# Two message layers of a graph network on one core: who waits for copied rows and added sums, when a half tile's own rows are copied, and where unused rows are cleared

## What is computed

```python
h = x @ W_enc.T + b_enc
row, col = (edge_index[0], edge_index[1])
for l in range(2):                                  # the two message layers
    m = jnp.concatenate([h[row], h[col]], axis=-1)
    m = jax.nn.relu(m @ msg_W1[l].T + msg_b1[l])
    m = m @ msg_W2[l].T + msg_b2[l]
    agg = jax.ops.segment_sum(m, col, num_segments=h.shape[0])
    upd = jnp.concatenate([h, agg], axis=-1) @ upd_W[l].T + upd_b[l]
    h = _layer_norm(h + upd, ln_g[l], ln_b[l])
return h @ W_out.T + b_out
```

## Time and profile before

| | |
|---|---|
| median of the runs | 3340.25 us |
| the profiled execution: span from its first to its last instruction | 3302.9 us |
| the median less that span (what lies around it) | 37.35 us |
| message layer 0, first and second pass | 626.3 to 911 us, 915.5 to 1254 us |
| message layer 1, first and second pass | 1360.7 to 1646 us, 1650.7 to 1990 us |
| TensorE matmuls busy | 2918.4 us (88%) |
| VectorE busy | 2503.1 us (76%) |
| ScalarE busy | 2057.0 us (62%) |
| GpSimd busy | 703.6 us (21%) |
| granted TensorE clock over the span | 0.934 of full speed |

### The profile page before, as it was taken

One profiled execution on the slowest core, in us unless ns is written; L12 is line 12 of the kernel. 1 busy time (PEld: TensorE's weight loads), 2 busy tenths in 40 slices (PEclk: granted clock), 3 DMA queues, 4 the chain that ended last, 5 costly groups with the idle time before them and its releaser, 6 DMA issues.

```text
span 3302.9 us, 219046 instructions
## 1 busy us (share of the span) xinstructions
PE 2918.4 (88%) x88775; PEld 2722.9 (82%) x88775; DVE 2503.1 (76%) x4764; ACT 2057.0 (62%) x3886; POOL 703.6 (21%) x909
## 2 busy tenths in 40 slices
PE   3666665799999998799999997799999899999999
PEld 3555454699989997699989996699999799999999
DVE  8999999777767776677777775689899855565555
ACT  1433333677767776777767774677777555555555
POOL 2222123400011117200011116244444300000000
PEclk7777776999999999899999998799999999999999
DMA  3000000566656762466667663155555488868888
GB/s 74 7 6 6 6 6 20 179 186 182 189 167 185 190 183 68 142 186 187 185 171 188 185 182 56 50 180 183 182 183 184 147 262 265 265 214 246 272 262 252
DMA packets 409174, 518.87 MB, mean 157 GB/s; under 512 B 157279, under 2 KB 280709, under 8 KB 409095
## 3 DMA queue, kind: packets, MB, share of 16 engines
q1 hardware_dynamic: 395757, 498.98, 51.0%
q0 software_dynamic: 4000, 8.20, 2.2%
q10 hardware_dynamic: 9338, 10.73, 1.1%
HBM read 408.98 MB, written 108.72 MB: 157 GB/s over the span
## 4 chain that ended last, share of the span: by engine, by line
PE 70%; DVE 13%; issue 7%; DMA 4%; POOL 3%; ACT 2%; SPq 0%; DVEq 0%; POOLq 0%; ACTq 0%
PE psum L1349 19%; PE psum L1583 17%; PE psum L1367 9%; PE psum L1353 9%; PE psum L1570 6%; PE psum L1550 3%; PE psum L703 1%; DMA tabf<-in_x 1%; PE psum L1558 1%; DMA cells_kept<-arena 1%; DVE Hf L943 1%; DVE Hf L1082 1%; DMA arena<-rows_far,ovcur 1%; DVE Hf L2144 1%; POOL arena L2057 1%
## 5 line engine op out<-in xcount | busy, mean ns | idle before, releaser
L1349 PE MATMUL psum<-tabf,arena 125*32 125x128 f16 x40256 | 1091.8, 220 | 27.9 <-DVE arena L1445 16.0
L1353 PE MATMUL psum<-arena 96*32 96x128 f16 x20928 | 1027.5, 221 | 7.4 <-issue 7.4
L1349 PEld LDWEIGHTS psum<-tabf,arena 125*32 125x32 f16 x40256 | 949.8, 98 | 91.4 <-issue 45.0
L1400 ACT ACTIVATE arena<-psum 128x512 f32<-128x512 f32 x1300 | 775.2, 596 | 340.4 <-PE psum L1353 339.5
L1353 PEld LDWEIGHTS psum<-arena 96*32 96x32 f16 x20928 | 690.5, 95 | 7.7 <-issue 7.7
L1583 PE MATMUL psum<-tabr,cellr 125*125 125x256 f32 x5000 | 623.4, 285 | 6.2 <-ACT cellr L1502 6.0
L1583 PEld LDWEIGHTS psum<-tabr,cellr 125*125 125x125 f32 x5000 | 606.4, 187 | 7.1 <-issue 7.1
L1367 PE MATMUL psum<-arena 128*32 128x129 f32 x10400 | 565.9, 277 | 1.4 <-issue 1.4
L1502 ACT CAST cellr<-arena 125x630 fp32r<-125x630 f16 x500 | 359.7, 720 | 267.4 <-PE psum L1583 255.8
L1502 DVE CAST cellr<-arena 125x630 fp32r<-125x630 f16 x500 | 244.0, 488 | 241.3 <-PE psum L1583 236.0
L1612 ACT CAST arena<-psum 125x500 f16<-125x500 f32 x625 | 356.6, 578 | 100.7 <-PE psum L1550 46.0
(11 more groups left out here) (313 smaller groups left out, 4444.9 us busy)
## 6 DMA issues: line engine op xcount, KB each, us to landing
arena<-cells_kept SPq DMA_DIRECT2D x500, 315.0 KB, 3.5
cells_kept<-arena SPq DMA_DIRECT2D x625, 126.0 KB
arena<-slots_turned_from SPq DMA_DIRECT2D x152, 384.0 KB
tabf<-slots_turned_from SPq DMA_DIRECT2D x150, 384.0 KB, 4.0
arena<-slots_turned_from SPq DMA_DIRECT2D x50, 512.0 KB
tabf<-slots_turned_from SPq DMA_DIRECT2D x50, 512.0 KB
arena<-slots_turned_to SPq DMA_DIRECT2D x152, 96.0 KB
tabf<-slots_turned_to SPq DMA_DIRECT2D x150, 96.0 KB, 4.3
```

The costliest lines, as they stand in the source:

```text
L1349: pe.matmul(psCell[b][q:q + GW, g * D:(g + 1) * D], fr, rows, start=g == 0 and p == 0, stop=False, tile_position=(0, q), skip_group_check= ...
L1353: m = pe.matmul(psCell[b][q:q + GW, g * D:(g + 1) * D], toB[part][:, here + q:here + q + GW], cur[:, part, g, :], start=g == 0 and 4 * k + ...
L1400: act.activation(msgs[:, SLOT[pos], :, 0:D], psCell[SLOT[pos]].rearrange("p (c d) -> p c d", d=D), ACT.Relu).then_inc(f_msg, 1)
```

## The change

Four things are edited:

1. TensorE no longer waits for the copied rows (`f_cur`) or for the sums (`f_add`). VectorE waits for `f_cur` between `toN` and `toB`, and for `f_add` ahead of `toE`; TensorE's remaining waits for `toB` and `toE` cover both. A gather's wait for `f_msg` is dropped, since an earlier scatter waited for the same relu.
2. ScalarE copies the second half's rows ahead of the relu of position 0 (was: after it), and the next tile's first-half rows after the relu of position 2 (was: after that of position 3).
3. `toB` and `cur` move in memory to where no other stage writes, and the 32 unused rows are cleared once, in `first_dve` ahead of message layer 0's tables, and no longer at the start of each message layer.
4. TensorE's wait for the clears becomes 4 and 5 in the two layers (was 4 and 8).

```diff
@@ memory @@
+        STAGE_USED = 2 * 2 * 128 + 3 * 2 * D + 3 * 2 * 2 * D + 3 * 2 * D
         toN = [carve([P, n * RG * CELL], F16) for n in SPAN]
+        toE = [carve([128, n, RG, GW]) for n in SPAN]
+        carve([128, STAGE_USED - sum(n * RG * CELL // 2 + n * RG * GW for n in SPAN)])
         toB = [carve([STACKED, n * RG * CELL], F16) for n in SPAN]
-        toE = [carve([128, n, RG, GW]) for n in SPAN]
-        cur = carve([STACKED, 2, RG, D], F16)
         ovrows = carve([128, CP, D], F16)
...
         msgs = carve([128, CELL_RING, RG, W + 1])
+        cur = carve([STACKED, 2, RG, D], F16)
@@ cells_pe @@
                     if at in (0, 3):
-                        half = part_of(at)
-                        pe.wait_ge(f_cur[half], i + (tiles_before(kk, half == 0) + tile + 1 + half))
-                        pe.wait_ge(f_toN, i * 2 + part_done(kk, tile, half))
-                    pe.wait_ge(f_msg, before_visit(i, kk, pos))
+                        pe.wait_ge(f_toN, i * 2 + part_done(kk, tile, part_of(at)))
...
                         pe.wait_ge(f_toE, i * 2 + marks_done(kk, 0, half))
-                        pe.wait_ge(f_add[half], i + (kk * (NT + half) + 1 + half))
...
-                pe.wait_ge(f_one, 4 * (l + 1))
+                pe.wait_ge(f_one, 4 + l)
@@ cells_act @@
                     for w in range(2):
+                        own_rows(1, w, None, i * (2 * n) + visit_done(w - 1, kk, n - 1, 2))
                         for pos in range(n):
...
-                            if pos == 0:
-                                own_rows(1, w, None, i * (2 * n) + visit_done(w - 1, kk, n - 1, 2))
-                            if pos == 3:
+                            if pos == 2:
                                 own_rows(0, 1 - w, ...
@@ cells_dve @@
                     dve.tensor_scalar(toN[half][:, span], slist[v][half][0][0:P, span], row1[0:P, :], None, ALU.is_equal)
+                    hold(dve, "dve", f_cur[half], i * 2 + (tiles_before(kk, half == 0) + w + tile + 1 + half))
                     dve.tensor_scalar(toB[half][0:CP * GW, span], slist[v][half][1][:, span], row32[:], None, ALU.is_equal).then_inc(f_toN, 1)
...
                     dve.wait_ge(f_sca, i * (2 * n) + visit_done(w + tile - 1, kk, part_end(kk, half)))
+                    dve.wait_ge(f_add[half], i * 2 + (kk * (NT + half) + w + tile + 1 + half))
...
-                if h == 0:
-                    for unused in (toB[0], cur, toB[1]):
-                        dve.memset(unused[CP * GW:STACKED], 0.0).then_inc(f_one, 1)
@@ first_dve @@
             dve.tensor_copy(AGG[:, :, D], selfs[0:P, 1:NT + 1])
+            dve.wait_ge(o_ST, SORTS)
+            for u in range(2):
+                dve.wait_ge(o_store[u], 32 * (SORTS // 2 + 1))
+            for unused in (toB[0], toB[1], cur):
+                dve.memset(unused[CP * GW:STACKED], 0.0).then_inc(f_one, 1)
             dve.wait_ge(s_root, 1)
```

## The result

| | before | after |
|---|---|---|
| median of the runs | 3339.72 us (3338.98 to 3342.28, 4 runs) | 3363.74 us (3352.98 to 3369.03, 4 runs) |
| ratio, 95% interval | | 1.0065 (1.0049 to 1.0082) |
| profiled execution: its span, its own time | 3302.9 us, unknown | 3362.4 us, 3364.19 us |
| two second passes, first to last scatter (before: 915.5 to 1258.1, 1650.8 to 1992.5) | 342.6 and 341.7 us | 376.6 and 372.1 us |

The change makes the kernel slower by about 24 us; 34.7 us faster was forecast. The size depends on the chip. On three other chips the kernel before ran in 3300.03, 3302.88 and 3305.56 us, and on the second of them the changed kernel took 3370.26, a ratio of 1.0203 (1.0187 to 1.0219). The profile of before, with its span of 3302.9, is like the executions there and not like the 3340 us runs: after, span and own time differ by 1.8 us, not by 37.

The account below looks back on a forecast made before the run. TensorE, busy 88% of the span, was taken as the bound. Terms -36 (waits), +5 (far rows), +2 (compares), -6.0 and +0.3 (clears) gave -34.7 us, from 3340.25 to 3305.5 us; range 3288 to 3328.

Parts of the forecast that it names:

- the one on the far rows: Second passes: the far rows' unshortened path limits every second tile's gain; loss 0 to 10 us, 5 taken.
- the stacked rows' DMAs: On SyncE, waiting for ScalarE's moved copy: they start earlier, costed at 0.
- the compare moves later: VectorE's `toB` behind ScalarE's copy: ready 0.26 us before TensorE's g3; 2 us lost, bounds 0 and 20.
- The lists' DMAs: They wait for `toB`, up to 0.5 us later, against a tile and more of lead: costed at 0.
- Its sign for this path: Second passes: weight loads would wait for the far rows' signal (L1318) in more than half of the 50 pairs.
- the slower one: Rival: VectorE's compare behind ScalarE's copy sets the pace, 0.1 us a tile in 200 tiles; 3354.5 us, chance 0.04.
- P: Follow-up theory, not in the prediction: while VectorE's compare runs, GpSimd's issue of the indirect DMA does not get on.
- D: Follow-up theory, not in the prediction: SyncE's transfers are under way when far rows' packets should start, and these wait.
- TensorE's waits: Fewer waits at the branch and around s0 save 0.18 us a tile in layer 0's first pass, 0.09 at each.
- satisfied waits are free: Rival: gaps belong to the branch and instruction fetching, so only the clears pay; 3334.5 us, chance 0.08.
- part 1: Waits taken off TensorE in the four message passes save 36 us, bounds 0 and 67.
- The clears: Start of each message layer: without clears TensorE's first gather comes 3.0 us earlier, 6.0 in all; moved clears lose 0.3.

Follow-up runs that it names:

- y1_order_as_before: Changed kernel with TensorE waiting for copied rows again and ScalarE's copies in the old order; 3278.57 us, ratio 0.9916.
- z2_fill: y1_order_as_before plus a useless VectorE compare between `toN` and `toB` in the second passes, so `toB` ends later; 3330.52 us.
- z1_best: y1_order_as_before with GpSimd's index copy for the next block made ahead of its wait; 3277.87 us, ratio 0.9920.
- z3_copies_back: Changed kernel with ScalarE's copies in the old order, the compare keeping its wait for them; 3438.12 us.
- y2_stack_late: Changed kernel with SyncE's stacked rows held until the tile's first scatter and the first-half copy back behind relu 3; 3568.18 us.
- x3_index_ahead: Changed kernel with GpSimd's index copy for the next block made ahead of its wait, issue 1.37 us earlier; 3294.0 us, ratio 0.9988.
- y4_before_copies_early: Kernel before with only ScalarE's copies in the new order, the compare staying where it was; 3356.81 us, ratio 1.0159.
- x1_pe_waits_copies: Changed kernel with the wait for copied rows back on TensorE and off VectorE; 3332.04 us, ratio 1.0095.
- x0_before: The kernel before, unchanged, run again for time and profile together; 3304.41 us, ratio 1.0003.

## Why the prediction was wrong

**The step that failed** is the one on the far rows: "This path isn't shortened, so every second tile can shorten only by its slack", with 0 to 10 us as bounds. The path was *lengthened*, by 1.7 us in the median of the 50 pairs of tiles. It had next to no slack: in the kernel before TensorE's gather started a median of 0.15 us behind the signal. Two sentences behind it costed the causes at nothing: that the stacked rows' DMAs "start earlier" (0), and that the compare moves later (judged only by when TensorE wants `toB`, with a margin of 0.26). Both moved into the window of GpSimd's issue and of its packets; the earlier trace rows had the issue and the compare next to each other, SyncE's issues stood in no row. The lists' DMAs were costed at 0 as well, as "up to 0.5 us later"; measured against the far rows' issue they came 0.68 us earlier, since SyncE issues them behind the stacked rows, and it is their packets that the far rows met. Its sign for this path came true, 48 pairs waiting where it wanted over half; what it had wrong is how long. No rival held it: the slower one was the compare setting the pace, and TensorE waited for the compare once.

By the 2 x 2 of the table, each run held against before on its own chip, early transfers alone cost 56 us, a late compare alone 49, both together 92, against the 24 us that the rest of the change gains. Why both cost less than their sum was not tried; the 92 also hold some 6 us of layer 1's first pass, which has no far rows. On the chip of the first comparison before is 40 us slower and after is not, which leaves 24; why was not settled, and no profile of before from that chip exists.

**P behind its rows.** In five kernels with the compare running as the issue starts, the issue ended 0.84 to 0.85 us behind the compare's end (medians of before, y1_order_as_before, the changed kernel, z2_fill, z1_best), and with no compare over it (z3_copies_back, most blocks of y2_stack_late) it took 0.97 in all. It isn't held up throughout: in x3_index_ahead the compare started 0.34 us behind the issue, ran for 1.28, and the issue needed only 0.13 more, so 0.84 of the 0.97 us that it takes alone were behind it by then. The Trainium skill ("SBUF — State Buffer", the paragraph on the "DVE blocks DMA" trap in the section on SBUF's two separate sides) says that GpSimd cannot write the descriptors of a DMA issued from its queue while VectorE runs an operation in a two-port mode. The runs agree in that the issue waits for this float16 compare of uint8 input; none shows the mode or the writing of descriptors. The prediction did not weigh it.

**D behind its rows.** The same issue of 1.21 us was followed by the first packet 0.7 us later with the list's packets behind it, 1.7 with them ahead. The Trainium skill ("DMA: Bandwidth & Descriptors", Queues, rings and completion order) says that each DMA engine takes turns between queues only after a whole packet of several descriptors. No run here shows the turn itself. What the records show is that the far rows' first packet came when a median of 68 of the list's 128 had started in y4_before_copies_early, and 104 in the changed kernel.

**What held.** TensorE's waits: forecast 0.18 us per first-pass tile, measured 0.16 in the rows. Its split was wrong: 0.12 of the 0.13 around s0 went (0.09 forecast), and only 0.02 of the 0.11 at the branch (0.09 forecast), so what makes that gap is still there without the wait and the register instruction.

The boundary at which "satisfied waits are free" was judged is misread: the earlier trace rows and the prediction call the scatter at 836.32 s3, and it is s2, with g5 behind it, which has no such waits (the branch is behind s5 at 839.05, and 2.73 us back from there are three positions). s3 is at 837.22, and g0 follows it at

```profile
837.45 0.30 PE L1349 MATMUL psum<-tabf,arena 125*32 125x128 f16 x8
```

That is 0.23 us, so it costs nothing there either, and the conclusion stands by luck.

In layer 1's first pass the changed kernel gained nothing: from s5 over the branch to s0 it took 0.21 us more than an ordinary position (before 0.13), in x3_index_ahead too, but not in x1_pe_waits_copies and y1_order_as_before (0.10). The gap at the branch itself stayed 0.31; what grew is g2 behind it. The wait on VectorE goes with it; how, was not tried.

The sum of part 1 was too high: y1_order_as_before, in which the waits for relus and sums are gone from TensorE and the one for copied rows is not, has 19 us less in the four passes than x0_before, not 36. 9 us of the difference are in the far rows, for which the weight loads wait 13.0 us instead of 4.4. The clears: forecast 3.0 us per layer, 2.1 to 2.8 off TensorE's idle time, and in the total not to be seen.

## What to carry to other kernels

An edit that lets a transfer or a compare start earlier or later is not free because its own consumer has time: write down what else runs in the new window. In this kernel the DMA issued by GpSimd was exposed twice, to VectorE's compare while it was issued and to another queue's large transfer ahead of its packets. Follow a moved issue down its engine's stream, too: here the small transfer that moved did no harm, and the large one behind it did. Where waits are to be taken from the bound engine, try each part alone: here the part without the reordering and without the moved wait for copies was worth 24 us, and the whole cost 67.

## What was not expected of the hardware

An indirect DMA of 128 rows takes GpSimd 0.97 us to issue with no compare over it, 1.21 with a compare's last 0.36 us over it, 1.80 to 1.88 with its last 0.95 to 1.04 us, and 1.75 with a whole compare (1.28 us) inside. A tiny copy on GpSimd (128 x 1) takes 0.18 us with VectorE idle (x3_index_ahead, z1_best), 0.33 beside the `toE` compare (z3_copies_back) and 0.59 beside `toN` (before). The far rows' first packet comes 0.72 us behind the issue's end, and 1.17 us or more behind it when packets of a 512 KB transfer of SyncE's queue are ahead. The same kernel, before, takes 3300.03, 3302.88 and 3305.56 us in three sets of runs and 3339.72 on another chip.
